# A perceiver block on one core: normalised rows replaced by centred rows, with the scale applied after the products

## The reference, cut to what matters

```python
def _layernorm(x, axis=-1, eps=1e-05):
    m = jnp.mean(x, axis=axis, keepdims=True)
    v = jnp.var(x, axis=axis, keepdims=True)
    return (x - m) / jnp.sqrt(v + eps)

x = x + _L0_xattn_ref(_layernorm(x), ctx, ...)   # quantised product with the context
x = x + _L0_attn_ref(_layernorm(x), ...)         # a Mamba layer: W_in, convolution, scan, W_out
x = x + _L0_ffn_ref(_layernorm(x), ...)          # x @ W_base.T + b_base + routed low-rank experts
x = x + _L1_xattn_ref(_layernorm(x), ctx, ...)   # cross-attention, Q = x @ Wq.T + bq
x = x + _L1_attn_ref(_layernorm(x), ...)         # grouped-query attention with rotary positions
x = x + _L1_ffn_ref(_layernorm(x), ...)          # permuted block-diagonal MLP with GELU
```

## Time and profile before

| | us |
|---|---|
| median of 3 runs | 390.81 (389.24 to 392.25) |
| profiled execution | 390.28 |
| its span, first to last instruction | 388.5 |

### The profile page before, as it was taken

The page is one execution under the profiler, slowest core; times in us unless marked ns, Lnnn a source line. Parts: engine busy times, 40 slices in busy tenths (PEclk is TensorE's granted clock), DMA queues, the critical chain, the costliest instruction groups (busy, mean ns, idle before and its releaser), DMA issues.

```text
span 388.5 us, 5274 instructions
## 1 busy us (share of the span) xinstructions
PE 356.5 (92%) x2054; PEld 231.9 (60%) x2054; DVE 269.0 (69%) x334; ACT 197.7 (51%) x397; POOL 115.3 (30%) x97
## 2 busy tenths in 40 slices
PE   0788999999999999999999999899999989999996
PEld 0335444653566666556655777688343567788785
DVE  2757057757887999998973777786820788975281
ACT  1980133169999697677710744463021279251160
POOL 2600000024999798889910000002000000310000
PEclk9999999999999999999999989999999999999999
DMA  6999999553002020254128798299999995000001
GB/s 251 423 424 392 352 420 345 213 197 128 2 3 109 0 90 19 94 189 156 56 108 283 272 412 349 93 347 345 365 422 401 416 426 214 2 2 2 0 2 54
DMA packets 12825, 81.34 MB, mean 209 GB/s; under 512 B 2094, under 2 KB 2350, under 8 KB 3519
## 3 DMA queue, kind: packets, MB, share of 16 engines
q1 hardware_dynamic: 11614, 78.23, 52.4%
q10 hardware_dynamic: 1154, 2.70, 2.1%
q0 software_dynamic: 32, 0.07, 0.0%
HBM read 80.34 MB, written 0.52 MB: 208 GB/s over the span
## 4 chain that ended last, share of the span: by engine, by line
PE 57%; DVE 16%; POOL 11%; issue 7%; DMA 6%; ACT 3%; POOLq 0%; SPq 0%; DVEq 0%; ACTq 0%
PE psum L1017 10%; PE psum L969 9%; PE psum L1137 7%; PE psum L1242 6%; DMA ring<-in_ctx 6%; PE psum L1093 5%; POOL arena L618 5%; PE psum L976 4%; PE psum L931 3%; PE psum L1161 3%; DVE arena L1595 2%; POOL arena L621 2%; PE psum L1361 2%; PE psum L1396 2%; POOL plain L618 2%
## 5 line engine op out<-in xcount | busy, mean ns | idle before, releaser
L768 ACT ACTIVATE arena<-arena 128x126 f32<-128x126 f32 x256 | 76.5, 387 | 9.7 <-DVE arena L1595 9.2
L1017 PE MATMUL psum<-ring,hT 128*128 128x512 f32 x128 | 60.7, 603 | 0.8 <-ACT hT L686 0.8
L1595 DVE TENSOR_TENSOR_SCAN arena<-arena,psum 128x1024 f32<-128x1024 f32 x24 | 54.2, 2273 | 3.2 <-PE psum L1093 3.0
L618 POOL TENSOR_TENSOR arena<-arena 128x1024 f32<-128x1024 f32 x20 | 47.2, 2359 | 5.4 <-DVE arena L1595 5.4
L1137 PEld LDWEIGHTS psum<-arena,ident 128*128 128x128 f32 x292 | 35.6, 192 | 13.8 <-issue 9.2
L1638 DVE TENSOR_TENSOR rounded<-ring,rounded 128x2048 fp32r<-128x2048 f32 x16 | 36.4, 2284 | 9.9 <-ACT rounded L795 9.9
L795 ACT ACTIVATE rounded<-ring 128x2048 fp32r<-128x2048 f32 x16 | 30.6, 1914 | 24.1 <-PE psum L976 14.7
L558 POOL TENSOR_TENSOR small<-small 128x1 f32<-128x1 f32 x6 | 3.3, 554 | 124.2 <-DVE small L1419 124.2
L1137 PE MATMUL psum<-arena,ident 128*128 128x128 f32 x292 | 37.3, 278 | 1.6 <-POOL arena L621 1.6
L1017 PEld LDWEIGHTS psum<-ring,hT 128*128 128x128 f32 x128 | 22.2, 190 | 27.1 <-issue 26.0
L1093 PE MATMUL psum<-plain 64*128 64x512 f32 x128 | 36.1, 641 | 1.7 <-DVE arena L1595 1.3
(11 more groups left out here) (209 smaller groups left out, 584.6 us busy)
## 6 DMA issues: line engine op xcount, KB each, us to landing
ring<-in_w_in SPq DMA_DIRECT2D x16, 1024.0 KB, 12.7
ring<-in_ctx SPq DMA_DIRECT2D x13, 1024.0 KB, 12.1
ring<-in_w_out SPq DMA_DIRECT2D x8, 1024.0 KB, 4.8
ring<-in_ctx_t SPq DMA_DIRECT2D x7, 1024.0 KB, 6.1
ring<-in_w_base SPq DMA_DIRECT2D x4, 1024.0 KB, 4.8
ring<-in_x_wk SPq DMA_DIRECT2D x4, 1024.0 KB, 6.5
ring<-in_a_wo SPq DMA_DIRECT2D x4, 1024.0 KB, 11.4
ring<-in_x_wq SPq DMA_DIRECT2D x3, 1024.0 KB, 8.9
```

The lines of the kernel that those rows point to most:

```text
L618: pool.tensor_tensor(state[s % STATES], state[s % STATES], c, ALU.mult).then_inc(prod_ready, 1)
L768: last = act.activation(to, of, ACT.Exp, scale=a_par[:, k, state_no:state_no + 1])
L1017: last = pe.matmul(psum[:, proj_bank(j), :], hT[:, k, :], slot(w_in + u)[:, k % UK, :], start=(k == 0), stop=(k == KT - 1))
L1595: dve.tensor_tensor_scan(state[s % STATES], dA[:, s % 3, :], psum[:, p:p + 2, :].rearrange("p a b -> p (a b)"), 0.0, ALU.mult, ALU.add).th ...
```

## The change

`x_updated` and `norm(n)` of boundaries 1 to 5 are replaced by three functions. `add_to_x` makes every addition a `scalar_tensor_tensor` that also puts out the sum of its half of x (`accum_out`, into `x_sum`); `bn_stats` still follows the first half. `center()` makes the mean from the two sums in one small instruction and writes h = x - mean, which waits for nothing from POOL. `variance(n)` does `bn_stats` of the second half, `bn_aggr` and the epsilon later on DVE, behind the parts of h that PE waits for and ahead of the next `low`. POOL's power goes to a column of its own for each norm.

1/deviation then comes in where a result leaves PSUM: in ACT's copy of the W_in result (`proj_copy`), in the logits and in the addition of the experts' layer, in the query's bias addition, in the keys and values and in the score factor (`a_scale`, one new small DVE instruction), and in both copies of the permuted x (`picked`). Since the result of the experts' layer is scaled as a whole, `b_base` is no longer a product: it is loaded to all partitions and added to x by two DVE instructions ahead of the gate, and `ones_row` and its memset go. The idle products ahead of the transposes go from 17 to 11 calls, from 4 (between the two bias products) to 4, from 11 to 4, from 12 to 5 and from 11 to 4. The first norm, ahead of the first layer, is as it was.

```diff
-        rstd = carve(small, 16, 1)
+        x_sum = carve(small, 53, 2)
+        mean = carve(small, 22, 1)
+        a_scale = carve(small, 23, 1)
+        rstd = carve(small, 89, 6)
...
-        b_base = arena[0:1, 20576:20576 + D]
-        ones_row = arena[0:1, 2112:2112 + P]
+        b_base = carve(arena, 20576, D)
...
-                pool.tensor_tensor(rstd, var_eps, minus_half[:, 0:1], ALU.pow).then_inc(rstd_ready, 1)
+                pool.tensor_tensor(rstd[:, n:n + 1], var_eps, minus_half[:, 0:1], ALU.pow).then_inc(rstd_ready, 1)
...
-                act.activation(proj[:, j % 3, :], psum[:, proj_bank(j), :], ACT.Copy).then_inc(proj_sb, 1)
+                if j == 0:
+                    act.wait_ge(rstd_ready, 2)
+                act.activation(proj[:, j % 3, :], psum[:, proj_bank(j), :], ACT.Copy, scale=rstd[:, 1:2]).then_inc(proj_sb, 1)
...
-                    act.dma_start(b_base, dram["b_base"]).then_inc(bias_in, 16)
+                    act.dma_start(b_base, dram["b_base"].to_broadcast([P, D])).then_inc(bias_in, 16)
...
             act.wait_ge(krot_ready, 1)
+            act.wait_ge(rstd_ready, 5)
             for r in range(GQ):
-                last = act.activation(krep[:, :, r, :], krot.rearrange("p (g d) -> p g d", g=HKV), ACT.Copy)
+                last = act.activation(krep[:, :, r, :], krot.rearrange("p (g d) -> p g d", g=HKV), ACT.Copy, scale=rstd[:, 4:5])
...
                 act.activation(to[:, :, 0:DH], psum[rows, 0, 256:512].rearrange("p (h d) -> p h d", h=HKV),
-                               ACT.Copy).then_inc(v_ready, 1)
+                               ACT.Copy, scale=rstd[rows, 4:5]).then_inc(v_ready, 1)
...
-            idle_products(4, 17)
+            idle_products(4, 11)
             transpose_h(1)
...
-            pe.wait_ge(bias_in, 48)
-            pe.wait_ge(ones_set, 1)
-            for nh in range(2):
-                pe.matmul(psum[:, nh, :], ones_row, b_base[:, UN * nh:UN * nh + UN], start=True, stop=False)
-                idle_products(3, 2)
+            idle_products(6, 4)
             transpose_h(2)
             for kh in range(2):
-                split_products(0, left_half, 4 + kh, UK * kh, False, False, unit_used, fresh=(hs_high, hs_low, kh + 1))
+                split_products(0, left_half, 4 + kh, UK * kh, kh == 0, False, unit_used, fresh=(hs_high, hs_low, kh + 1))
...
-            split_products(1, left_half, 6, 0, False, False, unit_used)
+            split_products(1, left_half, 6, 0, True, False, unit_used)
             split_products(1, left_half, 7, UK, False, False, unit_used, hook=first_experts)
             experts(1)
...
-            idle_products(3, 11)
+            idle_products(3, 4)
             transpose_h(3)
...
-            idle_products(5, 12)
+            idle_products(5, 5)
             transpose_h(4)
...
-            idle_products(0, 11)
+            idle_products(0, 4)
             transpose_h(5)
...
-                    dve.tensor_scalar(h[:, halves(nh)], x[:, halves(nh)], mv[:, 0:1], rstd, ALU.subtract,
+                    dve.tensor_scalar(h[:, halves(nh)], x[:, halves(nh)], mv[:, 0:1], rstd[:, 0:1], ALU.subtract,
                                       ALU.mult).then_inc(h_ready, 1)
...
-            def x_updated(ins):
-
-                ins.then_inc(x_ready, 1)
+            def add_to_x(nh, bank, factor=1.0):
+
+                dve.scalar_tensor_tensor(out=x[:, halves(nh)], in0=psum[:, bank, :], scalar=factor, in1=x[:, halves(nh)],
+                                         op0=ALU.mult, op1=ALU.add, accum_out=x_sum[:, nh:nh + 1]).then_inc(x_ready, 1)
                 updates[0] += 1
                 dve.wait_ge(x_ready, updates[0])
-                statistics((updates[0] - 1) % 2)
-
-            def add_to_x(nh, bank):
-                x_updated(dve.tensor_tensor(x[:, halves(nh)], x[:, halves(nh)], psum[:, bank, :], ALU.add))
+                if nh == 0:
+                    statistics(0)
+
+            def center():
+                step(dve.tensor_scalar(mean, x_sum[:, 0:1], x_sum[:, 1:2], 1.0 / D, ALU.add, ALU.mult))
+                for nh in range(2):
+                    dve.tensor_scalar(h[:, halves(nh)], x[:, halves(nh)], mean, None, ALU.subtract).then_inc(h_ready, 1)
+
+            def variance(n):
+
+                statistics(1)
+                dve.wait_ge(stats_ready, 2 * n + 2)
+                step(dve.bn_aggr(mv, stats.rearrange("p a b -> p (a b)")))
+                dve.tensor_scalar(var_eps, mv[:, 1:2], LN_EPS, None, ALU.add).then_inc(var_ready, 1)
...
-            def context_product(nh):
-
-                x_updated(dve.scalar_tensor_tensor(out=x[:, halves(nh)], in0=psum[:, nh, :], scalar=q_s12,
-                                                   in1=x[:, halves(nh)], op0=ALU.mult, op1=ALU.add))
...
                 context_offset(nh)
-                context_product(nh)
-
-
-            norm(1)
+                add_to_x(nh, nh, q_s12)
+
+
+            center()
...
             dve.wait_ge(hT_psum, 2)
             dve.tensor_copy(hT[:, 4:8, :], psum[:, 7, :]).then_inc(hT_hi, 1)
+            variance(1)
...
-            norm(2)
+            center()
             left_low(2)
+            variance(2)
             low(5)
             low(6)
             low(7)
+            dve.wait_ge(bias_in, 48)
+            for nh in range(2):
+                dve.tensor_tensor(x[:, halves(nh)], x[:, halves(nh)], b_base[:, halves(nh)], ALU.add).then_inc(biased, 1)
             dve.wait_ge(tri_in, 16)
             dve.wait_ge(ar_psum, 1)
             ranks = NE * RANK
-            step(dve.tensor_copy(logit, psum[:, 2, ranks:ranks + NE]))
+            dve.wait_ge(rstd_ready, 3)
+            step(dve.tensor_scalar(logit, psum[:, 4, ranks:ranks + NE], rstd[:, 2:3], None, ALU.mult))
             step(dve.tensor_reduce(top, logit, AX, ALU.max))
             dve.tensor_scalar(top, top, -1.0, None, ALU.mult).then_inc(top_ready, 1)
...
             low(8)
+            dve.wait_ge(biased, 2)
             for nh in range(2):
                 dve.wait_ge(base_psum, nh + 1)
-                add_to_x(nh, nh)
-
-
-            norm(3)
+                add_to_x(nh, nh, rstd[:, 2:3])
+
+
+            center()
             left_low(4)
+            variance(3)
             low(9)
             low(10)
             low(11)
...
             def query(nh):
                 dve.wait_ge(xq_psum, nh + 1)
-                dve.tensor_tensor(xq[:, halves(nh)], psum[:, nh, :], bq[:, halves(nh)], ALU.add).then_inc(xq_ready, 1)
+                if nh == 0:
+                    dve.wait_ge(rstd_ready, 4)
+                dve.scalar_tensor_tensor(out=xq[:, halves(nh)], in0=psum[:, nh, :], scalar=rstd[:, 3:4], in1=bq[:, halves(nh)],
+                                         op0=ALU.mult, op1=ALU.add).then_inc(xq_ready, 1)
...
                 dve.wait_ge(xatt_psum, nh + 1)
-                x_updated(dve.scalar_tensor_tensor(out=x[:, halves(nh)], in0=psum[:, 2 + nh, :], scalar=sinv,
-                                                   in1=x[:, halves(nh)], op0=ALU.mult, op1=ALU.add))
-
-
-            norm(4)
+                add_to_x(nh, 2 + nh, sinv)
+
+
+            center()
             left_low(6)
+            variance(4)
             low(17)
             low(18)
...
             low(23)
+            dve.wait_ge(rstd_ready, 5)
+            step(dve.tensor_scalar(a_scale, rstd[:, 4:5], ASCALE, None, ALU.mult))
             for r in range(GQ):
                 dve.wait_ge(as_psum, r + 1)
                 v = aprob[:, r, :, :]
-                step(dve.scalar_tensor_tensor(out=v, in0=psum[:, r, :].rearrange("p (j s) -> p j s", j=HKV), scalar=ASCALE,
+                step(dve.scalar_tensor_tensor(out=v, in0=psum[:, r, :].rearrange("p (j s) -> p j s", j=HKV), scalar=a_scale,
                                               in1=wide(mask, HKV), op0=ALU.mult, op1=ALU.add))
...
 
-            norm(5)
+            center()
             left_low(10)
+            variance(5)
             dve.wait_ge(g_psum, 2)
-            dve.tensor_copy(picked[:, halves(1)], psum[:, 5, :]).then_inc(picked_hi, 1)
+            dve.wait_ge(rstd_ready, 6)
+            dve.tensor_scalar(picked[:, halves(1)], psum[:, 5, :], rstd[:, 5:6], None, ALU.mult).then_inc(picked_hi, 1)
```

More of the change, by code:

```diff
@@ L842, in _ @@
             act.wait_ge(gT_psum, 1)
-            act.activation(lora_gT, psum[:, 3, 0:P], ACT.Copy).then_inc(gT_ready, 1)
+            act.activation(lora_gT, psum[:, 5, 0:P], ACT.Copy).then_inc(gT_ready, 1)
             high(9)
@@ L911, in _ @@
             act.wait_ge(g_psum, 1)
-            act.activation(picked[:, 0:UN], psum[:, 4, :], ACT.Copy).then_inc(picked_lo, 1)
+            act.wait_ge(rstd_ready, 6)
+            act.activation(picked[:, 0:UN], psum[:, 4, :], ACT.Copy, scale=rstd[:, 5:6]).then_inc(picked_lo, 1)
             act.wait_ge(gT_turned, 1)
@@ L1195, in _ @@
             for k in range(KT):
```

(10 more changed lines are left out.)

6 lines of the change are left out of this document (2 added, 4 removed).

## The result

| | before | after |
|---|---|---|
| median, us | 390.6 (4 runs) | 383.94 (383.86 to 384.01, 3 runs) |
| profiled execution, us | 390.28 | 383.87 |
| its span, us | 388.5 | 382.1 |
| mean clock granted to TensorE | 0.996 | 0.999 |

The ratio is 0.984, with an interval of 0.982 to 0.987: the change makes the kernel faster by 1.3 to 1.8%. One further execution of the changed kernel took 879.33 us, at a clock of 1.00; nothing on record explains it, and it is left out. In a second set with more executions the times were 383.97 (383.87 to 384.09, 6) and 389.78 (11), the ratio 0.984 again.

The account below looks back on a forecast made before the run. PE was taken to wait first on the path to h, then on `low`'s place in DVE's queue. 1.41 + 1.02 + 0.25 + 1.25 + 1.39 - 0.25 = 5.07 us off 390.28, plus 0.53 to the median: 385.7, range 383.9 to 388.6.

Parts of the forecast that it names:

- forecast case: The prediction's main case: 385.7 us, with its own range of 384.6 to 387.0, chance 0.68.
- scores: Ahead of the first scores: the new `a_scale`, 0.21 + 0.04, puts 0.25 us on the path.
- The path to h: Boundaries 1 to 5: last addition to h shrinks to 1.11 us; the gains at h sum to 6.84.
- The first rival: The accumulating addition takes 0.53 us longer each on the path, 4.5 in all, time 390.2; chance 0.08.
- What `variance` gives back: Statistics ahead of the next `low` lose 1.14 us at boundaries 2 and 3, 0.14 at 4, nothing at 1 and 5.
- The clock at boundary 2: Without bias products, h to the second subtraction's end takes 3.22 us at full clock, not 4.12: 0.90 gained.
- The bias and the multiplications: Bias additions ahead of the logits cost nothing, the gate being 0.46 us early; DVE's factors keep lengths within 0.06.
- The idle products: Ahead of the transposes: seven calls fewer are 1.67 us, none on the path; boundary 3 idles 0.98 against 0.69.
- the falling clock: Rival: clock falls behind the shortened idle products at boundaries 1, 3, 4, 5, 1.5 us each, time 392.6; chance 0.04.
- The loads: Rival: `a_wkv` lands at its old time, ending the first three boundaries' gains (2.68 us) there, time 388.4; chance 0.06.

Follow-up runs that it names:

- Experiment 7: Changed kernel with `variance` behind the first `low` instead of ahead of it, at boundaries 2 and 3 only: 382.67 us, ratio 0.981 to the kernel before.
- experiment 4: Kernel before with the changed kernel's fewer idle products (11, 4, 5 and 4 at boundaries 1, 3, 4 and 5): 392.95 us, ratio 1.007.
- experiment 3: Changed kernel without any idle products at all five boundaries: 387.81 us, ratio 0.994 to the kernel before.

## Why the prediction was right, and where its sizes were off

385.7 was forecast and 383.94 measured, 0.04 above the lower end of the range, 383.9, and below the forecast case's own 384.6: the path was right, but that the number lies inside is in part luck. The gain was put too low. Between the two profiled executions the change gives 6.41, against a sum of 5.07. Term by term, from the same anchors in both traces (at a boundary, from the last addition to x to the unit of PE that follows):

| | predicted | measured |
|---|---|---|
| boundary 1 | 1.41 | 1.63 |
| boundary 2 | 1.02 | 1.45 |
| boundary 3 | 0.25 | 0.49 |
| boundary 4 | 1.25 | 1.59 |
| scores | -0.25 | -0.29 |
| boundary 5 | 1.39 | 1.57 |
| between them | 0 | -0.03 |

**The path to h** was the right mechanism and the main term. Its tail was put at 1.11 and is 0.98 to 1.05, since the accumulator read of 0.08, which I added in full, overlaps the addition; at boundaries 1, 2 and 4 I had also charged 0.08 or 0.14 for the first addition. The two halves of h became shorter as well, which I hadn't priced: they take 0.88 together against 1.00 (483 against 543 ns on average), now with one operation and one operand from memory instead of two.

**The first rival**, a slow accumulating addition, is refuted: it takes 0.68 or 0.69 without a factor and 0.75 with one, as before. The Trainium skill's rule on two SBUF sources, named in the prediction, is not tested by this, since one source is in PSUM. What the Trainium skill says of such an instruction elsewhere ("VectorE: DVE Perf Modes", Two Vector instructions with no wait between them), that it is two, the main one and an accumulator read, agrees with the trace, which shows the read as a row of its own with 0.08.

**What `variance` gives back** was right in place and 0.19 too large. It was summed from whole durations, 1.14, but consecutive instructions of DVE overlap: between the subtraction's end and the start of `low` lie 0.95. At boundary 4 I charged 0.14 and it was nothing, since `high(17)` moved with h and covers it. Experiment 7 confirms the mechanism: with `variance` behind the first `low`, PE's unit comes 1.05 earlier at boundary 2.

**The clock at boundary 2** was the wrong kind of term. I read 0.90 from one execution as a property of the kernel. It is one of part of the executions: the trace that I summed against had the fall, 22 of 52 had none. Between the profiled executions the 0.90 was 0.96, as forecast. Against an execution of before without a fall, 389.3, the change gives 5.4, which the sum without this term puts at 4.17, and boundary 2 gives 0.57, which it puts at 0.12. The removal of the one-row products takes the 390 class away; the median gets from it only what the mix of executions makes. Why none of nine executions of the changed kernel falls into the 391 class either is not shown.

**The bias and the multiplications.** The gate had its cover, 0.88 and not 0.46, since I had summed whole durations here too: from h to the logits DVE needs 11.91 (221.08 to 232.99) and not 12.56. Experiment 7 shows the cover gone: PE is 0.20 late. The scores cost 0.29 and not 0.25. `a_scale` is 0.15 long instead of 0.21, but the four score instructions are 0.06 longer each, which I had called "within 0.06" and left out of the sum. In DVE's queue that makes 0.42 (5.17 ahead at the `low` before them, 4.75 at the last reduction behind them). PE feels `a_scale` and the first two: at the second and third group of transposes behind the scores it is 4.88 ahead (339.10 to 334.22, 340.61 to 335.73).

**The idle products.** "None of them is on the path" holds in the new kernel with its new counts. What the prediction argued against the falling clock, that 0.69 of idleness at boundary 3 did no harm, was no measure of longer pauses: with pauses of 2.1 to 2.3 it fell at four of four boundaries (experiment 4). The price of such a fall, 1.5 us, was too high: 0.7 to 0.9 were measured. The changed kernel has pauses of 0.73 at most, so the rival didn't come true.

**The loads** moved, by 3.5 us at `a_wkv`, and that rival is refuted.

## What to carry to other kernels

Where a small chain stands between a result and the next matrix work, look first at which of its parts the next product needs, and put the rest behind it: here the mean was needed at once and the deviation only where results leave PSUM. Then follow the moved work to the next thing in its queue, since at boundary 3 two thirds of the gain at h were lost there. And take the filler of a wait down together with the wait: here fewer fillers alone cost 2.6 us, and the shorter wait alone left 2.6 us unused.

## What the hardware showed that I had not expected

- POOL's power on 128 x 1 numbers takes 0.55 or 0.57 alone and 2.52 to 2.58 beside DVE's `low` (boundaries 2, 3 and 4), which has two inputs in SBUF. It ends 0.40 after the first `low` of boundary 2 does, as if it had been kept out for that instruction. Nobody waits for it there, so it costs nothing; in the kernel before, DVE stood still while POOL did it.
- The clock's answer to a pause is not a function of its length alone: 1.56 at boundary 5 was followed by a fall to 0.66, 1.86 at boundary 4 by none (experiment 3, one trace). What decides between them stays open.
- The kernel before falls into four classes of time, 389.3, 390.4, 391.0 and 392.4, and its median moves with the mix: 390.6 in the first set and 389.78 in the second. Nine executions of the changed kernel lie within 0.23 us of each other.
